# A gated cross-attention block with routed experts: the additions to the output wait for a product, and five steps stand later

## The chip, the cores and the metric

The kernel runs on one core of one Trainium2 chip. The metric is the device time of one execution in microseconds (us), as the median of several runs. The engines of the core work from queues of their own: TensorE (PE, whose weight loads are shown as PEld), VectorE (DVE), ScalarE (ACT), GpSimd (POOL) and SyncE (SP); they meet through semaphores. POOL and SP also issue the transfers (DMA).

## The reference, cut to what matters

32 batches of 112 rows of width 256 (3584 rows) go through two layers. In the first, each row looks at 375 context rows and at the normed rows themselves (8 heads of 64), and the result, times a gate, is added to x. In the second, each row is normed and sent to 2 of 8 experts, and the result, times a gate, is added too:

```python
x = x + jnp.tanh(g_xattn[0]) * xattn(ctx_1024, layernorm(x), mask, ...)
h = layernorm(x)
bids = sigmoid(h @ conf_w.T + conf_b) * wealth
top_bids, selected = jax.lax.top_k(bids, 2)            # 2 of E = 8 experts
weights = softmax(top_bids)
def ffn(gw, uw, dw):                                   # (1024,256), (1024,256), (256,1024)
    return (silu(h @ gw.T) * (h @ uw.T)) @ dw.T
x = x + jnp.tanh(g_ffn[0]) * sum(weights[e] * ffn_e(h) for the chosen e)
```

## The kernel before, in words

**Two stages.** The first 32 rounds (some 840 us) are the attention, one batch a round. The second stage is the experts' layer, which starts at about 855 us and is the one that the change touches. Its rows were scattered by expert into a buffer in HBM (`routed_rows`) and are taken up again in NT = 63 tiles of 128 rows. Each engine walks through the same loop `for t in range(1, NT + 1): step(t, ...)`, unrolled, each in its own written order; nothing but semaphores ties the engines together, and no planner moves anything.

**Precision by splitting.** A float32 matrix is held as two float16 halves (`hi` by ACT, `lo` by DVE), and `product` makes three matmuls for each block (hi·hi, hi·lo, lo·hi).

**One tile on PE** (`step`, L1792). `act_T(t-1, 1)` transposes the second half of the last tile's activations into `aP`; `tile_T(t+1)` transposes the next tile's rows into `xP`; `gate_up(t, q, 0)` makes the gate product and then the up product of the first 512 inner columns with the weights held in the array (48 matmuls of 128 columns, "weights held", tile names `gP<-xT,W` and `uP<-xT,W`); `gate_up(t, q, 1)` makes the other 512 inner columns with the rows held (12 matmuls of 512 columns, `gP<-W,xT` and `uP<-W,xT`, "the wide products"); `down(t-1)` makes the down product of the tile before (24 matmuls of 256 columns, `yP`). `gate_up(t, q, i)` adds one to `s_gu` at the end of its up product, so `s_gu` is 2t+1 after the products with weights held of tile t, and 2t+2 after the wide ones.

**Beside it.** In ACT's and DVE's step t stand, in this order: the hi and lo halves of the last tile's second activation half (`act_hi` L901, `act_lo` L1411, tile `aT<-aP`), of the next tile's rows (`tile_hi` L891, `tile_lo` L1396), then silu and the gated product of half 0 (`silu` L895, `gated` L1401), hi and lo of half 0 (`aT<-act_h`), silu and gated product of half 1. DVE then weighs the down product's rows (`weigh` L1417, tile `ysb`). POOL adds them to the output in HBM by an indirect, adding DMA (`add_tile` L637, DMA at L641). In POOL's step t the addition is that of tile t-1; `weigh(t-1)` comes after `down(t-1)` of PE's step t, so POOL's step t is worked through while PE is in its tile t+1. Before the addition POOL waits until the addition before it has landed (`s_add`, L668) and then issues the load of the rows of tile t+4 (`load_tile` L582, DMA at L587).

**The experts' weights.** They are loaded raw (float32, six pieces of 512 KB for an expert, `raw`), POOL issuing them in its steps after the addition: for experts 2 to 7 two pieces in each of three steps, those with t % 5 of 4, 0 and 1 (`FREE_AT`, `next_raw` L530). From the fifth expert on the split weights are also written to HBM (`put_pieces` L524). At the end of its steps ACT squares the pieces to find their size (`expert_squares` L845, tile `junk`): piece 0 in the step with t % 5 = 0, pieces 1 and 2 in the next, 3 to 5 in the one after. In the step with t % 5 = 3 PE sums the squares over the partitions (`expert_sums` L1651, `bP`), DVE makes a bound of them (`expert_bound` L1242), POOL takes the power -1/2 (`expert_pow` L518, `epow`), DVE makes the scale (`expert_scale` L1248), and ACT and DVE then split the pieces (`expert_hi` L856, `expert_lo` L1260, tile `W<-raw`).

**The start of the stage** (`tail`, L1694): PE works the first tile's products in between the last batch's output product, its norm's transposes (`norm2_T` L1626) and its routing confidences (`confidences` L1632). Tile 5 (the sixth; AHEAD = 5) is loaded only once the routing table is there, so its transposes stand later in step 4 than those of other tiles.

Matmuls are helper calls: line 1542 is `product`, 1773 `act_T`, 1737 `tile_T`, 1655 `expert_sums`.

Of the kernel before, what the change touches and what calls it, by code (L numbers as in the profile page):

```python
# [54 lines left out]
AHEAD = 5  # L55
# [35 lines left out]
def build(nc, x, ctxt, mask, scal, lnw, wqkv, wout, confw, confbw, wffn, out):  # L91
# [4 lines left out]
    with ctx:  # L96
# [220 lines left out]
        def holds(b, lo, hi):  # L317

            return lo <= b <= hi if isinstance(b, int) else True
# [121 lines left out]
        def _(pool):  # L441
# [76 lines left out]
            def expert_pow(p):  # L518

                pool.wait_ge(s_ech, p * ECHAIN + 2)  # L520
                apart(pool)
                nc.gpsimd.tensor_tensor(epow[:, :], ebound[:, :], minus_half[:, 0:3], ALU.pow).then_inc(s_epow, 1)
# [121 lines left out]
            def step(t, k):  # L644
# [30 lines left out]
                if p < E and t % SPAN == 3 and p > 1:  # L675
                    expert_pow(p)
                if holds(t, 1, NT):
                    add_tile(t - 1, (t - 1) % XT_BUFS)
# [21 lines left out]
        def _(act):  # L700
# [210 lines left out]
            def step(t, k):  # L911
# [17 lines left out]
                if t == AHEAD - 1:  # L929
                    tile_hi(t + 1, 1 - q)  # L930
                if t < NT:
                    if 0 not in TURNED:
                        act_hi(t, q, 0)
                    silu(t, 1, place)
                    if 0 in TURNED:
                        act_hi(t, q, 0)
# [30 lines left out]
        def _(dve):  # L967
# [455 lines left out]
            def step(t, k, place, last_place):  # L1423
# [13 lines left out]
                if t == AHEAD - 1:  # L1437
                    tile_lo(t + 1, 1 - q)
# [4 lines left out]
                if p < E and j == 3 and p > 1:  # L1443
                    expert_bound(p, bP)
                if t < NT:
                    gated(t, 1, place)
                    if 0 in TURNED:
                        act_lo(t, q, 0)
# [4 lines left out]
                if p < E and j == 3 and p > 1:  # L1453
                    expert_scale(p)
# [80 lines left out]
        def _(pe):  # L1535
# [158 lines left out]
            def tail():  # L1694
# [16 lines left out]
                gate_up(0, 0, 1, 0, (0,))  # L1711
                norm2_T(B - 1, (B - 1) % 4)
                gate_up(0, 0, 1, 0, (1,))
# [78 lines left out]
            def step(t, k, byte, last_byte):  # L1792
# [9 lines left out]
                if t == AHEAD - 1:  # L1802
                    tile_T(t + 1, (t + 1) % XT_BUFS)
                if SPAN < t and t // SPAN + 1 < E and t % SPAN == 3:
                    expert_sums(t // SPAN + 1, bP)
                if t == 1:
                    gate_up(t, q, 1, byte, (0,))
                    ranks(QUADS - 1, B * H, last_rank_P, last_tot_P)
                    gate_up(t, q, 1, byte, (1,))
                elif t < NT:  # L1810
                    gate_up(t, q, 1, byte)
                place = next_byte = None
# [60 lines left out]
```

## Time and profile before

| what | value |
| --- | --- |
| median of 3 runs | 1436.99 us (1432.22 to 1437.5) |
| the profiled execution | 1435.85 us, its span 1434.3 us |
| busy share of the span | PE 94%, PEld 68%, DVE 71%, ACT 65%, POOL 34% |
| mean granted TensorE clock | 0.989 of full speed |
| chain that ended last | PE 70%, DVE 10%, ACT 6%, issue 6%, DMA 5% |
| experts' stage, 960 to 1190 us | PE busy 226.17 of 230 us, DVE 138.54, ACT 135.04, POOL 87.76 |
| same, 1190 to 1250 us | PE busy 60.00 of 60 us |

The span is the stretch that the trace covers; the execution's own time is 1.55 us longer. In the rows, an x with a number gives how many instructions a row merges; what stands in brackets is the idle time of the engine before the row, and what ended it. "issue" is idle time for which the profile shows no releaser.

### The profile page before, as it was taken

The page shows a single profiled execution, that of the slowest core. Times are in us where ns is not written, and L with a number is a line of the kernel's source. Part 1 is how long each engine was busy: PE and PEld are TensorE (multiplying, and loading weights), DVE is VectorE, ACT ScalarE, POOL GpSimd, SP SyncE. Part 2 cuts the span into 40 slices and gives each one's busy share as a digit, 9 for nine tenths or more (in the row PEclk, how much of TensorE's full clock was granted, in tenths as well). Part 3 has the DMA queues.
Part 4 walks back from the last instruction along what each step waited for, and adds up shares of the span by engine and source line. Part 5 has one row for each costly group of instructions (what it writes and reads, how often), then busy time and mean ns, then how long its engine had stood idle before and what let it go on. Part 6 is the DMA issues. An engine that isn't in the chain of part 4 may idle for free.

```text
span 1434.3 us, 41525 instructions
## 1 busy us (share of the span) xinstructions
PE 1351.1 (94%) x13880; PEld 969.2 (68%) x13880; DVE 1023.5 (71%) x2528; ACT 934.8 (65%) x1932; POOL 488.2 (34%) x659
## 2 busy tenths in 40 slices
PE   2999999999999999999999979999999999999996
PEld 1466666666666666666665657688878778887784
DVE  4688888888888888888888776566556654444442
ACT  5687878787787878878787765566656663333331
POOL 4423322433433334334333143433344333222221
PEclk9999999999999999999999979999999999999998
DMA  4010101111111111111112146433376753112461
GB/s 119 27 42 26 42 23 29 52 40 49 34 53 30 41 46 39 49 33 53 31 33 96 41 129 196 107 98 93 98 211 178 228 152 94 31 31 35 120 203 16
DMA packets 56913, 109.26 MB, mean 76 GB/s; under 512 B 10832, under 2 KB 34768, under 8 KB 56720
## 3 DMA queue, kind: packets, MB, share of 16 engines
q0 software_dynamic: 23712, 55.71, 15.2%
q1 hardware_dynamic: 32160, 49.86, 11.2%
q8 instruction: 126, 2.06, 0.6%
q10 hardware_dynamic: 848, 1.07, 0.3%
q14 instruction: 67, 0.55, 0.1%
HBM read 69.16 MB, written 37.45 MB: 74 GB/s over the span
## 4 chain that ended last, share of the span: by engine, by line
PE 70%; DVE 10%; ACT 6%; issue 6%; DMA 5%; SPq 1%; POOL 1%; POOLq 0%; DVEq 0%; ACTq 0%
PE fP L1542 19%; PE yP L1542 10%; PE uP L1542 10%; PE gP L1542 10%; PE simP L1590 5%; PE ptP L1600 4%; PE tP L1542 3%; PE oP L1542 3%; DVE ms L1036 3%; DVE pT L1042 2%; DMA out<-ysb,xt 2%; PE aP L1773 2%; DVE ao L1054 1%; ACT z L732 1%; PE fP L1558 1%
## 5 line engine op out<-in xcount | busy, mean ns | idle before, releaser
L1542 PE MATMUL fP<-zTs,ws 128*128 128x112 f16 (+1 forms) x1536 | 220.3, 294 | 8.7 <-DVE zTs L1378 5.3
L1542 PE MATMUL fP<-ws,zTs 128*128 128x512 f16 x768 | 186.8, 379 | 0.5 <-DVE kT L1026 0.2
L1036 DVE CUSTOM_DVE_ANT_0 ms<-simP,madd,sim_undo 112x488 f32<-112x488 f32 x256 | 183.9, 720 | 3.3 <-PE simP L1590 1.3
L769 ACT ACTIVATE pr<-ms,nmax 112x488 f32<-112x488 f32 x256 | 179.0, 699 | 3.3 <-DVE nmax L1036 0.5
L1042 DVE SCALAR_TENSOR_TENSOR pT<-ptP,pT 122x448 f16<-122x448 f32 x256 | 157.8, 616 | 28.0 <-ACT pT L776 27.3
L1542 PEld LDWEIGHTS fP<-zTs,ws 128*128 128x128 f16 x1536 | 109.8, 99 | 99.7 <-issue 34.9
L1542 PE MATMUL yP<-W,aT 128*128 (+1 forms) x1512 | 175.4, 273 | 1.8 <-DVE aT L1414 1.8
L1542 PEld LDWEIGHTS yP<-W,aT 128*128 128x128 f16 x1512 | 147.6, 98 | 32.8 <-issue 2.5
L1408 DVE SCALAR_TENSOR_TENSOR act_h<-uP,consts,sg 128x512 f32<-128x512 f32 x126 | 94.5, 750 | 103.1 <-ACT sg L899 102.7
L776 ACT ACTIVATE pT<-ptP 122x448 f16<-122x448 f32 x256 | 137.8, 538 | 40.8 <-PE ptP L1600 39.7
L899 ACT ACTIVATE sg<-gP,consts 128x512 f32<-128x512 f32 x126 | 86.5, 686 | 114.6 <-PE uP L1542 114.4
L641 POOL DMA_INDIRECT out<-ysb,xt x63 | 105.2, 1670 | 157.4 <-DVE ysb L1421 143.8
L1542 PE MATMUL oP<-v,pT 122*128 122x64 f16 x3072 | 133.6, 194 | 14.0 <-DVE pT L1042 9.1
L1600 PE MATMUL ptP<-ident,pr 112*122 112x112 f32 x1024 | 142.0, 261 | 0.4 <-DVE filled L1148 0.4
L499 POOL TENSOR_TENSOR zTs<-zT,zTs 128x1200 f16<-128x1200 f32 x31 | 76.5, 2469 | 193.1 <-ACT zTs L750 193.1
L1542 PEld LDWEIGHTS oP<-v,pT 122*128 122x128 f16 x3072 | 121.0, 98 | 26.6 <-DVE pT L1042 26.5
L1600 PEld LDWEIGHTS ptP<-ident,pr 112*122 112x122 f32 x1024 | 114.2, 139 | 25.6 <-issue 0.8
L1542 PEld LDWEIGHTS fP<-ws,zTs 128*128 128x128 f16 x768 | 67.9, 98 | 82.1 <-issue 14.4
L1590 PE MATMUL simP<-kT,qT 64*128 64x488 f16 x768 | 102.7, 372 | 13.3 <-DVE nmax L1036 12.4
L1026 DVE SCALAR_TENSOR_TENSOR kT<-fP,kT 128x488 f16<-128x488 f32 x128 | 84.9, 664 | 37.2 <-ACT kT L762 37.2
L762 ACT ACTIVATE kT<-fP 128x488 f16<-128x488 f32 x128 | 73.8, 576 | 51.4 <-PE fP L1542 51.3
L1026 DVE SCALAR_TENSOR_TENSOR v<-fP,v 122x512 f16<-122x512 f32 x128 | 88.3, 690 | 26.5 <-ACT v L762 26.0
(233 smaller groups left out, 2496.2 us busy)
## 6 DMA issues: line engine op xcount, KB each, us to landing
raw<-wffn POOLq DMA_DIRECT2D x36, 512.0 KB, 6.9
split_experts<-W POOLq DMA_DIRECT2D x12, 1024.0 KB, 10.0
W<-split_experts SPq DMA_DIRECT2D x16, 768.0 KB, 7.9
xc<-ctxt SPq DMA_DIRECT2D x32, 375.0 KB
xt<-routed_rows POOLq DMA_DIRECT2D x63, 129.0 KB, 2.4
raw<-wffn SPq DMA_DIRECT2D x12, 512.0 KB, 9.5
routed_rows<-padrows SPq DMA_DIRECT2D x8, 645.0 KB, 7.9
xl<-x SPq DMA_DIRECT2D x32, 112.0 KB
```

Of the source, the lines that this page charges most:

```text
L499: nc.gpsimd.tensor_tensor(zTs[p][:, 1, :, :], zT[:, :, :], zTs[p][:, 0, :, :], ALU.subtract).then_inc(s_zsplit, 1)
L641: pool.indirect_dma_start(out[:, :], bass.IndirectOffsetOnAxis(ap=xt[k][:, D:D + 1].bitcast(I32), axis=0), ysb[t % 2][:, :], None, compute ...
L769: nc.scalar.activation(pr[h % 2][:, :], ms[h % 2][:, :], ACT.Exp, bias=nmax[p][:, h:h + 1], scale=-1.0, accum_out=rsum[p][:, h:h + 1]).the ...
L776: nc.scalar.activation(pT[h % 2][:, 0, :, 0:S], ptP[h % 2][0:KR, :, 0:S], ACT.Copy, scale=P_TOP).then_inc(s_pthi, 1)
L899: nc.scalar.activation(sg[i][:, :], gP[i][:, :], ACT.Silu, scale=constant(place, 0)).then_inc(s_silu, 1)
L1026: nc.vector.scalar_tensor_tensor(out=o, in0=i, scalar=1.0 / TOP, in1=hi, op0=ALU.mult, op1=ALU.subtract).then_inc(s_plo, 1)
L1036: nc.vector.tensor_tensor_reduce(out=ms[h % 2][:, :], in0=simP[h % 2][0:S, 0:NK], in1=madd[p][:, :], scale=sim_undo[0:S, 0:1], scalar=3.0e ...
L1042: nc.vector.scalar_tensor_tensor(out=pT[h % 2][:, 1, :, 0:S], in0=ptP[h % 2][0:KR, :, 0:S], scalar=P_TOP, in1=pT[h % 2][:, 0, :, 0:S], op0 ...
L1408: nc.vector.scalar_tensor_tensor(out=act_h[i][:, :], in0=uP[i][:, :], scalar=constant(place, 2), in1=sg[i][:, :], op0=ALU.mult, op1=ALU.mu ...
L1542: last = nc.tensor.matmul(o, lhs(k, a), rhs(k, c), start=n == 0, stop=n == len(todo) - 1)
L1590: last = nc.tensor.matmul(simP[i][:, 0:NK], qT[p][r, a, h // 2, :], kT[p][r, c, h // 2, :], start=t == 0, stop=t == len(PARTS) - 1)
L1600: last = nc.tensor.transpose(ptP[h % 2][0:KR, c, 0:S], pr[h % 2][:, c * KR:(c + 1) * KR], ident[0:S, 0:S])
```

## The change

- POOL, in its steps 6 to 61, waits before the addition of tile t-1 until `s_gu` is 2(t+1)+1, that is, until the up product with weights held of tile t+1 has ended.
- The sums of an expert's squares (`expert_sums`, experts 2 to 7) stand behind the wide products of PE's step instead of ahead of them; the bound (`expert_bound`) stands behind the second gated product of DVE's step, right ahead of the scale.
- In step 4 the transposes of tile 5, and their hi and lo halves on ACT and DVE, stand behind the wide products, the second silu and the second gated product.
- At the start of the stage the transposes of the last batch's norm stand behind all of `gate_up(0, 0, 1, 0)` instead of between its gate and its up product.

```diff
@@ POOL, step @@
                 if p < E and t % SPAN == 3 and p > 1:
                     expert_pow(p)
+                if AHEAD < t < NT - 1:
+                    pool.wait_ge(s_gu, (t + 1) * 2 + 1)
                 if holds(t, 1, NT):
                     add_tile(t - 1, (t - 1) % XT_BUFS)
@@ ACT, step @@
-                if t == AHEAD - 1:
-                    tile_hi(t + 1, 1 - q)
                 if t < NT:
                     if 0 not in TURNED:
                         act_hi(t, q, 0)
                     silu(t, 1, place)
+                    if t == AHEAD - 1:
+                        tile_hi(t + 1, 1 - q)
@@ DVE, step @@
-                if t == AHEAD - 1:
-                    tile_lo(t + 1, 1 - q)
                 if t < NT and 0 not in TURNED:
                     act_lo(t, q, 0)
                 if t == 2:
                     tile_places()
-                if p < E and j == 3 and p > 1:
-                    expert_bound(p, bP)
                 if t < NT:
                     gated(t, 1, place)
+                    if t == AHEAD - 1:
+                        tile_lo(t + 1, 1 - q)
...
                 if p < E and j == 3 and p > 1:
+                    expert_bound(p, bP)
                     expert_scale(p)
@@ PE, tail @@
                 gate_up(0, 0, 0, 0, (1,))
-                gate_up(0, 0, 1, 0, (0,))
+                gate_up(0, 0, 1, 0)
                 norm2_T(B - 1, (B - 1) % 4)
-                gate_up(0, 0, 1, 0, (1,))
                 confidences(B - 1)
@@ PE, step @@
                 if 1 < t < NT:
                     gate_up(t, q, 0, byte)
-                if t == AHEAD - 1:
-                    tile_T(t + 1, (t + 1) % XT_BUFS)
-                if SPAN < t and t // SPAN + 1 < E and t % SPAN == 3:
-                    expert_sums(t // SPAN + 1, bP)
...
                 elif t < NT:
                     gate_up(t, q, 1, byte)
+                if t == AHEAD - 1:
+                    tile_T(t + 1, (t + 1) % XT_BUFS)
+                if SPAN < t and t // SPAN + 1 < E and t % SPAN == 3:
+                    expert_sums(t // SPAN + 1, bP)
```

## Rows read from the trace of the kernel before

**Rows 1.** The table of waits, 900 to 1430 us: total us, times, longest.

```profile
ACT junk L854 <- DMA raw<-wffn: 31.2, 19, 4.7
PE bP L1655 <- ACT junk L854: 3.2, 3, 1.4
```

**Rows 2.** The timeline of tiles 22 and 23: start us, length us, engine, line, what.

```profile
1056.73 0.60 PE L1773 MATMUL aP<-ident,act_h 128*128 128x128 f32 x4
1057.39 1.50 PE L1542 MATMUL gP<-xT,W 128*128 128x128 f16 x24
1058.46 1.66 POOL L641 DMA_INDIRECT out<-ysb,xt  x1 [0.95 <-DVE ysb L1421]
1058.73 1.50 PE L1542 MATMUL uP<-xT,W 128*128 128x128 f16 x24
1059.23 1.06 ACT L854 ACTIVATE junk<-raw 128x1024 bf16<-128x1024 f32 x1 [3.20 <-DMA raw<-wffn]
1059.51 1.74 POOL L534 DMA_DIRECT2D raw<-wffn  x2
1060.07 1.46 PE L1542 MATMUL gP<-W,xT 128*128 x6
1060.29 0.58 ACT L909 ACTIVATE aT<-aP 128x512 f16<-128x512 f32 x1
...
1065.28 0.60 PE L1773 MATMUL aP<-ident,act_h 128*128 128x128 f32 x4
1065.54 0.56 POOL L587 DMA_DIRECT2D xt<-routed_rows  x1 [3.58 <-issue]
...
1067.69 1.06 ACT L854 ACTIVATE junk<-raw 128x1024 bf16<-128x1024 f32 x1 [2.79 <-DMA raw<-wffn]
```

**Rows 3.** The timeline of tile 31 and the start of tile 32.

```profile
1137.66 0.60 PE L1773 MATMUL aP<-ident,act_h 128*128 128x128 f32 x4
...
1142.68 0.58 ACT L909 ACTIVATE aT<-aP 128x512 f16<-128x512 f32 x1
...
1147.17 0.63 PE L1773 MATMUL aP<-ident,act_h 128*128 128x128 f32 x4 [0.28 <-issue]
```

**Rows 4.** The timeline of tile 8 (starts at 934.33) and tile 9: the power and the scale.

```profile
936.06 1.65 POOL L641 DMA_INDIRECT out<-ysb,xt  x1 [2.94 <-DVE ysb L1421]
...
941.18 0.57 POOL L587 DMA_DIRECT2D xt<-routed_rows  x1 [3.47 <-issue]
...
942.71 0.17 DVE L1251 TENSOR_SCALAR ebits<-epow 128x3 int32<-128x3 int32 x1 [0.36 <-POOL epow L522]
...
943.24 0.60 PE L1773 MATMUL aP<-ident,act_h 128*128 128x128 f32 x4
...
946.26 0.57 ACT L909 ACTIVATE aT<-aP 128x512 f16<-128x512 f32 x1
```

**Rows 5.** A window: us, busy PE, PEld, DVE, ACT, POOL, granted clock, DMA, GB/s.

```profile
901.50:904.50 3.00, 3.00 (x8) 1.06 (x7) 0.91 (x2) 0.27 (x1) 2.24 (x2) 0.50 0.54 92
```

**Rows 6.** The timeline of steps 4 and 5, around the sixth tile.

```profile
900.40 0.44 PE L1737 MATMUL xP<-ident,xt 128*128 128x128 f32 x2 [2.85 <-DMA xt<-routed_rows]
...
902.26 1.48 POOL L522 TENSOR_TENSOR epow<-ebound,minus_half 128x3 f32<-128x3 f32 x1
...
906.54 0.16 DVE L1251 TENSOR_SCALAR ebits<-epow 128x3 int32<-128x3 int32 x1
...
912.23 0.69 DVE L1414 TENSOR_TENSOR aT<-aP,aT 128x512 f16<-128x512 f32 x1
```

**Rows 7.** The groups by line, 840 to 1434 us: busy us, mean ns, idle before.

```profile
L1542 PE MATMUL uP<-xT,W 128*128 128x128 f16 x1512 | 99.1, 219 | 0.0
L1542 PE MATMUL gP<-xT,W 128*128 128x128 f16 x1512 | 96.7, 221 | 0.0
```

**Rows 8.** The timeline of POOL and PE in tile 30.

```profile
1132.46 1.46 PE L1542 MATMUL gP<-W,xT 128*128 x6
...
1132.84 1.60 POOL L641 DMA_INDIRECT out<-ysb,xt  x1 [0.30 <-issue]
```

## The prediction, made before the changed kernel was run

> **What bounds the kernel now.** I read the busy shares first, then the windows of the experts' stage: there PE has work nearly all the time (the table above: 226 of 230 us, then 60 of 60). So in this stage the time is PE's work plus what little PE waits, and a step is worth only what it takes from or adds to that. Then the timeline of one tile after another. An ordinary tile on PE is 8.55 to 8.7 us: from the transposes of `aP` to the products with weights held 0.66, gate 1.34 (1057.39 to 1058.73), up 1.34 (in other tiles to 1.5), the two wide products 2.59 and down 2.62 (together 1060.07 to 1065.28) [rows 2]. The table of waits has hardly a PE row: 3.2 us behind ACT's squares, three times [rows 1]. But ACT waits 31.2 us, 19 times, for the raw weights [rows 1]. That is the wait to watch, since ACT's squares stand ahead of the halves that PE's next down product needs.
>
> How late may ACT be? Tile 31 shows it: `aT<-aP` starts 5.02 us after the tile's start on PE, the tile lasts 9.51 instead of 8.57, and the next `aP` starts 4.49 after ACT's row [rows 3]. In between lie, one behind the other, ACT's halves and silu, DVE's gated product, the halves of half 0 and the second gated product; so PE stands still from a lateness of 8.57 - 4.49 = 4.1 us on, and each us above costs a us. In tile 22 the lateness is 3.56 [rows 2] and nothing stalls. I call this number the lateness of a tile.
>
> **Part 1, the wait ahead of the addition.** Before, the addition starts 1.73 us into the tile (1058.46) [rows 2], within the up product with weights held. Now it waits for that product's end, 3.34 into the tile. The start behind a semaphore took 0.8 us here when DVE's `ysb` was what it waited for, and PE's end is seen 0.15 us later; so 4.3 us, 2.6 later than now. POOL's queue behind it is: the raw pieces, the write of split weights, the wait for the landing, the load of rows for tile t+4, the power. The load of rows has three tiles to spare and costs nothing. POOL's own round fits: addition to load is 7.1 us in the fullest tiles (1058.46 to the load at 1065.54, [rows 2]), in a tile of 8.6.
>
> What it can gain: the addition's 1.65 us lie on the up product now. Counted by groups, up with weights held is busy 99.1 us and gate 96.7 [rows 7], 2.4 apart; by the distances of starts the 51 undisturbed up products of tiles 7 to 61 take 1.34 to 1.62 against 1.34, 4.3 us in sum, some of it with a full overlap at 1.34. In the wide products an addition costs nothing, by the one tile where it fell there: 1.46 as always [rows 8]. Gain between 0 and 4.3, taken as 3. The Trainium skill, "SBUF — State Buffer", section "SBUF: two separate sides", says that engine ports and DMA ports are disjoint, so that neither slows the other; by it this gain would be 0 and the sum 3 us higher. The trace leaves it open: up takes 1.34 in tile 22 under a whole addition [rows 2], and up to 1.5 in other tiles.
>
> What it costs, first: raw pieces. They start 1.05 us behind the addition (1059.51), so 5.4 into the tile instead of 3.0 or 2.8 (3.5 to 4.8 in four tiles where they are late today). The piece that is waited for lands 5.4 to 8.2 us after its issue (1059.51 to 1067.69, [rows 2]; 5.4 to 6 where no split weights are written), and ACT squares it as soon as it is there: in tile 22 it waited 3.20 for it and began `aT<-aP` 1.06 later [rows 2]. Every such lateness grows by 2.0 to 2.6 us. The pattern stands 18 times (six experts, three tiles each); lateness before and shift, with the stall of the tile ahead taken off where it lets the piece come earlier in the tile:
> - tile 8: 2.7 + 2.6 = 5.3, stall 1.2; tile 13: 1.8 + 2.6, 0.3; tile 18: 2.5 + 2.6, 1.0;
> - tile 21: 3.0 + 2.0, 0.9; tile 22: 3.56 + 2.5 - 0.9, 1.1; tile 23: 4.7 + 2.6 - 1.1 = 6.2, 2.1, of which 1.5 are there now;
> - tile 26: 3.0 + 2.4, 1.3; tile 28: 4.8 + 2.5, 3.2, of which 1.6 now;
> - tile 31: 5.0 + 1.1, 2.0, of which 0.95 now; tile 33: 4.1 + 1.8, 1.8, of which 0.9 now; the other eight nothing.
> Sum 1.2 + 0.3 + 1.0 + 0.9 + 1.1 + 0.6 + 1.3 + 1.6 + 1.05 + 0.9 = 10 us.
>
> Second: the power waits on POOL for the landing of the addition in the same tile. Now 936.06 to the load at 941.18 is 5.1, to DVE's `ebits` 942.71 another 1.5 [rows 4]. From 4.3 this gives 10.9 into the tile instead of 8.4. The scale, ACT's three splits and DVE's two follow, and lateness of tile 9 is 946.26 - 943.24 = 3.02 [rows 4]. Less the length that the tile ahead has gained, it grows by 1.0 to 2.4 in the six tiles behind a scale: stalls of 0.75 (tile 9), 1.3, 0.9, 1.1, 0.95, 0.9, together 5.9 us.
>
> **Part 2, sums and bound later.** The sums go from ahead of the wide products to behind them; the 0.2 us of their two matmuls stay. PE's three waits of 1.1, 1.4 and 0.7 us there [rows 1] go, but the same late ACT holds the down product after them, so they are in the "now" of tiles 23, 28 and 33 above and not taken twice. The bound comes after the second gated product, 8.1 into the tile (0.35 long), and is there before POOL is free at 10.0; only in stalled tiles does it decide, which is in the 5.9. Cover gone: DVE no longer has 0.75 us of gated product beside the power, and waits; what is behind it is `weigh` (needed by the next down product, 3 us of air). In itself 0; if POOL were free it would cost 0.75 x 6 = 4.5 at most, and at best the sums give back their 3.2.
>
> **Part 3, the sixth tile.** PE waits 2.85 us for the rows of tile 5, [rows 6], and after that the granted clock is 0.50 [rows 5], so that the wide products take 2.2 and 2.1 instead of 1.3 each (six matmuls in 1.3 in tile 22, [rows 2]). Moved, the wide products run in the wait, and the transposes start at 900.40 as the load lands, whatever PE did before. Step 5 would begin at 900.40 + 0.27 + 2.62 = 903.3 instead of 907.57. What is late next is the power at 902.26 to 903.74 [rows 6], bound to POOL: `ebits` comes at 903.8 instead of 906.54, 2.8 earlier, and DVE's `aT<-aP` of 912.23 comes at 909.5, 6.2 into step 5. It stalled nothing at 4.7, so PE gives back 1.4. Gain 2.8; at least 1.5 if PE's shorter wait halves the clock once more, at most 4.3.
>
> **Part 4, the last norm later.** PE idled before these transposes and now works the up product in that time, about 1.5 us. But all PE steps up to 900.40 end in the wait for the sixth tile's load, and that hangs on SP's and POOL's transfers, not on PE. So 0; were that cover gone, 1.5 gained.
>
> **The last tiles.** POOL's steps 62 and 63 don't wait; the addition before them lands 1 us ahead of its need. 0.
>
> **Sum.** 1435.85 + 10 + 5.9 - 3 - 2.8 = 1446. The profiled execution lies 1.1 us below the median of the three runs, so the median may be 1446 to 1447; I say 1446.
>
> **Rivals.**
> - *The raw weights come in time* (faster). If landing is set by the transfers and not by the issue, later pieces meet emptier queues and land when they did; the power too has room. Then only the gains stay: 1435.85 - 3 - 2.8 = 1430. For it: pieces beside a write of split weights took 8.2 us, others 5.4 to 6, so traffic matters. Against it: the addition's neighbours shift with it, so the crowd shifts too, and in experts 2 to 4 there is no crowd. It decides from where landing takes 2.5 us less than now. The Trainium skill, "DMA: Bandwidth & Descriptors", section "Anatomy of one DMA — SWDGE (gpsimd) path", gives 2.0 us plus bytes / 436e3; for 512 KB that is an estimate of 3.2 us, with which no piece would be late and this rival would hold. The trace speaks against it: 8.2 us [rows 2].
> - *Half of it*: the limit of 4.1 is taken from one tile; if 0.5 more is in it, the 16 stalls lose 8 us: 1438.
> - *Nothing moves*: the wait is mostly met, additions start as before; 1436 - 2.8 = 1433. Against it: 1.73 is 1.6 ahead of the product's end [rows 2].
> - *The clock falls in the new stalls*: PE stands 1.3 to 1.4 us twice in tile 28. Waits of 1.1 and 1.4 [rows 1] were followed by wide products of 1.3, that of 2.85 by the clock of 0.50 [rows 5, 6]. If three stalls do, at 1.7 each as in step 4: 1451.
>
> **Chances.** Stalls as worked out, with or without the clock: 0.60 (of it 0.08 with). Half: 0.15. In time: 0.15. Nothing moves: 0.10. About 0.5%, 7.2 us, is what can be told from no change. Slower by more: most of the first case, 0.53; within: half and nothing, and the ends of both others, 0.33; faster: 0.14. Range 1431 to 1452; that of the likeliest alone 1442 to 1452.
>
> **What would show it.** Additions at 4.3 us into tiles 7 to 62; raw pieces at 5.4; ACT's waits for raw grown from 31 to some 60 us; tiles 8, 18, 21, 22, 26, 28 longer by 1 us and more, the tiles behind a scale by 0.8 to 1.3; up with weights held at 1.34 throughout; tile 40 and later shorter by 0.1 each; step 5 at 903.3. It is wrong if ACT's wait for raw does not grow, or the late tiles keep 8.6 us.

## The result, and the profile after

| | before | changed kernel |
| --- | --- | --- |
| median | 1435.69 us (1432.22 to 1437.5, 5 runs) | 1456.66 us (1455.9 to 1457.71, 5 runs) |
| ratio | | 1.0143 [1.0129, 1.0157] |
| profiled execution | 1435.85 us, span 1434.3 | 1455.9 us, span 1454.0 |
| PE busy, 960 to 1190 us | 226.17 of 230 | 222.31 of 230 |
| granted clock over the span | 0.989 | 0.992 |

The change is slower by 21 us; I had forecast 10, with a range up to 1452. In kernel.py the lines behind L676 carry numbers up to two higher than before. The table of waits of the changed kernel, 900 to 1450 us (total us, times, longest), answers [rows 1]:

```profile
POOL out L641 <- PE uP L1543: 145.3, 47, 7.0
...
ACT junk L856 <- DMA raw<-wffn: 55.3, 20, 5.1
...
PE yP L1543 <- DVE aT L1416: 7.0, 8, 1.5
...
PE aP L1773 <- DMA W<-split_experts: 1.9, 1, 1.9
PEld bP L1656 <- ACT junk L856: 0.9, 3, 0.4
```

The wait is real (47 additions now wait for `uP`), ACT's wait for raw weights grew from 31.2 to 55.3 us, and PE's waits for the squares are gone. But PE's own waits sum to about 12 us, those it had before included, and the span grew by 20. The timeline of tile 22 (starts at 1065.19), which answers [rows 2] and [rows 3], shows the rest:

```profile
1065.19 0.63 PE L1773 MATMUL aP<-ident,act_h 128*128 128x128 f32 x4 [0.28 <-issue]
...
1065.87 1.74 PE L1543 MATMUL gP<-xT,W 128*128 128x128 f16 x24
...
1067.50 1.97 PE L1543 MATMUL uP<-xT,W 128*128 128x128 f16 x24
1068.88 1.06 ACT L856 ACTIVATE junk<-raw 128x1024 bf16<-128x1024 f32 x1 [3.56 <-DMA raw<-wffn]
1069.37 1.46 PE L1543 MATMUL gP<-W,xT 128*128 x6
...
1070.37 1.66 POOL L641 DMA_INDIRECT out<-ysb,xt  x1 [3.19 <-PE uP L1543]
...
1071.42 1.74 POOL L534 DMA_DIRECT2D raw<-wffn  x2
...
1074.58 0.60 PE L1773 MATMUL aP<-ident,act_h 128*128 128x128 f32 x4
```

From gate to up is 1.63 us and from up to the wide gate product 1.87, where tile 22 of before had 1.34 and 1.34, and PE is busy all the while: the tile is 0.84 longer without a stall. The same in tile 10, behind the first late scale (`ebits` 2.1 us into tile 9 instead of 8.4 into tile 8; this answers [rows 4]):

```profile
942.14 0.57 POOL L587 DMA_DIRECT2D xt<-routed_rows  x1 [3.47 <-issue]
...
943.74 0.17 DVE L1253 TENSOR_SCALAR ebits<-epow 128x3 int32<-128x3 int32 x1 [1.93 <-POOL epow L522]
...
947.29 0.57 ACT L911 ACTIVATE aT<-aP 128x512 f16<-128x512 f32 x1
...
950.93 0.74 DVE L1410 SCALAR_TENSOR_TENSOR act_h<-uP,consts,sg 128x512 f32<-128x512 f32 x1
...
951.77 0.63 PE L1773 MATMUL aP<-ident,act_h 128*128 128x128 f32 x4 [0.23 <-issue]
...
952.46 1.80 PE L1543 MATMUL gP<-xT,W 128*128 128x128 f16 x24
...
954.15 2.03 PE L1543 MATMUL uP<-xT,W 128*128 128x128 f16 x24
...
956.07 1.46 PE L1543 MATMUL gP<-W,xT 128*128 x6
```

Tile 9 keeps my rule (lateness 947.29 - 941.63 = 5.66, length 10.14 = 5.66 + 4.48). Tile 10 has no late row at all and is 9.51 long instead of 8.66. What is different is where DVE's second gated product ends: 951.67, 0.10 us before PE's `aP`; in an undisturbed tile it is 0.94 to 0.95 before. I call that distance the lead. The groups by line, 840 to 1454 us, answer [rows 7]: up with weights held grew by 7.7 us, gate by 3.6.

```profile
L1543 PE MATMUL uP<-xT,W 128*128 128x128 f16 x1512 | 106.8, 218 | 0.9 <-issue 0.7
...
L1543 PE MATMUL gP<-xT,W 128*128 128x128 f16 x1512 | 100.3, 220 | 0.1
```

The sixth tile, against [rows 5] and [rows 6]: the window's granted clock is 1.00 now, the transposes start at 901.27, and step 5 at 904.86 instead of 907.57.

```profile
900.00:904.50 4.50, 3.97 (x29) 2.66 (x28) 1.98 (x4) 1.59 (x3) 3.46 (x4) 1.00 0.41 95
```

```profile
901.27 0.44 PE L1737 MATMUL xP<-ident,xt 128*128 128x128 f32 x2
...
903.23 1.48 POOL L522 TENSOR_TENSOR epow<-ebound,minus_half 128x3 f32<-128x3 f32 x1
...
904.74 0.17 DVE L1253 TENSOR_SCALAR ebits<-epow 128x3 int32<-128x3 int32 x1 [1.61 <-POOL epow L522]
904.86 0.60 PE L1773 MATMUL aP<-ident,act_h 128*128 128x128 f32 x4
```

### The profile page after: what moved, and what is told of

Its sections match the earlier page's. It is cut to its first block and busy times, and to the rows that moved or that the text cites. A ratio compares the mean times of both kernels' runs of the same rounds, so it can differ in the third digit from the quotient of the medians.

```text
span 1454.0 us, 41531 instructions
## 1 busy us (share of the span) xinstructions
PE 1365.2 (94%) x13880; PEld 975.1 (67%) x13880; DVE 1021.5 (70%) x2528; ACT 931.5 (64%) x1932; POOL 486.8 (33%) x659
## 5 line engine op out<-in xcount | busy, mean ns | idle before, releaser
L1543 PEld LDWEIGHTS yP<-W,aT 128*128 128x128 f16 x1512 | 147.0, 98 | 39.0 <-issue 10.3
L1591 PE MATMUL simP<-kT,qT 64*128 64x488 f16 x768 | 101.9, 369 | 13.4 <-DVE nmax L1038 10.6
L1543 PE MATMUL uP<-xT,W 128*128 128x128 f16 x1512 | 106.8, 218 | 0.9 <-issue 0.7
L1028 DVE SCALAR_TENSOR_TENSOR v<-fP,v 122x512 f16<-122x512 f32 x128 | 88.2, 689 | 26.5 <-ACT v L764 26.4
```

Of the source, the lines that this page charges most:

```text
L1028: nc.vector.scalar_tensor_tensor(out=o, in0=i, scalar=1.0 / TOP, in1=hi, op0=ALU.mult, op1=ALU.subtract).then_inc(s_plo, 1)
L1543: last = nc.tensor.matmul(o, lhs(k, a), rhs(k, c), start=n == 0, stop=n == len(todo) - 1)
L1591: last = nc.tensor.matmul(simP[i][:, 0:NK], qT[p][r, a, h // 2, :], kT[p][r, c, h // 2, :], start=t == 0, stop=t == len(PARTS) - 1)
```

## The experiments

Times stand beside those of before on the same chip. "Excess" is the length of tiles 7 to 35 above 8.55 us each, from distances of starts on PE in the profiled execution: 10.3 before, 29.3 after.

### Which part of the change costs: the wait

**e1**: before with the wait alone.

```
                 if p < E and t % SPAN == 3 and p > 1:
                     expert_pow(p)
+                if AHEAD < t < NT - 1:
+                    pool.wait_ge(s_gu, (t + 1) * 2 + 1)
```

> The kernel before with the new wait alone (POOL's steps 6 to 61 wait for the next tile's up product with weights held before the addition); nothing is moved. Theory (A): the wait alone makes raw pieces and power late, and a late ACT costs twice: the tile lasts lateness + 4.49 us, and where the second gated product is ready less than 0.3 us before PE takes it up, the next tile's products with weights held take some 0.85 us more. Then this run carries the whole loss of the change and lacks the 2.7 us that its step 4 gains: 1456 to 1460 us, some 19 tiles with weights-held products of 3.4 us and more instead of 2.7 to 2.8. Rival (B): the later sums and bound are what costs: 1446 or less, as forecast for the wait's own part.

Measured 1464.02 us against 1436.6, ratio 1.0196 [1.0168, 1.0225], excess 32.9; that is above the 1456 to 1460 that I expected, and made up otherwise: besides the tiles in which PE waits for squares, 7 of tiles 7 to 35 have held products above 3.3 us, not the 19 expected. ("Held products" are the gate and up products with weights held, both together.) The sums ahead of the wide products turn late squares into PE waits (13.1 us in the table of waits, 3.2 before), and in tiles 23, 28 and 33 the clock falls behind them. In tile 23 PE waits from 1079.8 to 1082.4, and the wide products take 2.48 and 1.79 us instead of 1.29 each. The window behind the wait has a granted clock of 0.62 (columns as in [rows 5]):

```profile
1077.94 1.89 PE L1544 MATMUL uP<-xT,W 128*128 128x128 f16 x24
1082.42 0.39 PE L1657 MATMUL bP<-esq,ones 128*128 128x6 f32 x2 [2.59 <-ACT junk L856]
1082.67 2.69 PE L1544 MATMUL gP<-W,xT 128*128 x6
1085.15 1.95 PE L1544 MATMUL uP<-W,xT 128*128 x6
```

```profile
1082.50:1087.00 4.50, 4.50 (x15) 1.79 (x16) 2.66 (x6) 1.83 (x4) 0.96 (x2) 0.62 0.34 62
```

So beside the wait the other parts together save about 7 us.

**e2**: the changed kernel without the wait (the two added lines of e1 taken out).

> The changed kernel without the new wait; sums, bound, sixth tile and last norm stand later. (A): step 4 gives 2.7 us; raw pieces start at 1.7 + 1.1 into the tile again. The bound now ends 8.5 us into the tile, so the scale comes about 1 us later than before in six tiles, lateness 3.0 grows to 4.0 to 4.4 there: stalls of 0 to 0.3 and a slow next tile each, 3 to 6 us in all. 1434 to 1440. (B): 1446 or more.

Measured 1438.17 against 1436.6, ratio 1.0012 [0.9999, 1.0026], excess 11.2. So nearly all of the 21 us are the wait's: 18.5 by the medians, 18.8 by the ratios.

**e9** and **e11**, and further down **e13** and **e14**: the changed kernel with fewer waits, by the condition on the wait:

```
e9:  if AHEAD < t < NT - 1 and (t % SPAN == 3 or t > 35):
e11: if 35 < t < 52:
e13: if AHEAD < t < 36 and t % SPAN == 2:
e14: if AHEAD < t < 36 and t % SPAN in (4, 0, 1):
```

> After, with the wait kept only in the 33 steps where neither a raw piece of weights nor the power of a scale is queued behind the addition or behind its landing: steps 8, 13, 18, 23, 28, 33 (tiles 9, 14, ... 34) and steps 36 to 61. Theory A (the wait costs only by what is queued behind it): as the kernel without the wait, 1438.2, plus up to 0.5 us per expert for raw pieces that come 0.4 us later and up to 2 us at tiles 60-61, where the reload of the last expert's place meets it: 1438 to 1442. Rival W (the wait costs by itself, or the late landing does through the tile's rows): the 18.5 us of 56 waits shared out evenly are 0.33 us for each, 33 of them 11 us: 1447 to 1450.

> After, with the wait only in steps 36 to 51 (tiles 37 to 52). In after and in the kernel with 33 waits tile 60 is 10.7 and 10.1 us long, with PE waiting 1.4-2.0 us for the reload of the eighth expert's place. Theory T (late additions in the last tiles beside the reload slow it): with no waits from step 52 on, tile 60 is back at 8.7 and the kernel stands at 1438 as without any wait, so 16 waits cost nothing. Rival (what makes the reload late lies further ahead): tile 60 stays over 10 us and the time is 1440.

e9: 1437.7 against 1436.29, ratio 1.001 [0.9996, 1.0025]; e11: 1437.41 beside 1438.02 (one run). A late addition costs nothing where nothing is queued behind it, and gains nothing either: tiles 36 to 59 together are 1.6 us above 8.55 each in before and 1.9 in the changed kernel. That the last tiles suffer from it did hold for e11 (tile 60 at 8.67), but e12 and e13 below have no wait there and tile 60 at 9.88 and 9.82, e16 10.69. Whether the reload of the eighth expert's place comes in time varies without the wait; the +2.2 us of that kind in the changed kernel's profile are not shown to be its doing.

**e13** and **e14**: the wait only in the six steps ahead of a scale, and in the 18 with raw pieces.

> After, with the wait only in steps 7, 12, 17, 22, 27, 32 (tiles 8, 13, 18, 23, 28, 33), where the power of the scale is taken behind this addition's landing and no raw piece is behind it. Theory A (the late landing makes the scale late): ebits 1.3-3 us into tiles 9, 14, 19, 24, 29, 34 instead of 0.4-1.0, those tiles 0.5 to 2 us longer than without the wait, 6 to 8 us in all, 1444 to 1446.5. Rival (the scale is late by the raw pieces' lateness, so this wait alone does little): 1438 to 1441.

> After, with the wait only in the 18 steps up to 35 whose raw pieces of weights are issued behind the addition (t mod 5 = 4, 0, 1; tiles 10-12, 15-17, ... 35). Theory A (the costs of the wait are two separate ones, and add up: 18.5 in all, 10.8 in the steps ahead of a scale, 0 in the quiet tiles): 1443 to 1448, raw pieces at 5.4 us, the squares late in tiles 11-13, 16-18, 21-23, 26-28, 33 as in after, ebits in tiles 9, 14 back at 0.4 us. Rival (they are one: the raw pieces' lateness costs only where the scale is late as well): 1438 to 1441.

e13: 1450.27 against 1438.02, ratio 1.0087 [1.0063, 1.0111], excess 22.5; e14: 1453.17 against 1435.81, ratio 1.0115 [1.0093, 1.0136], excess 26.4. Both cost more alone than I expected, and both rivals fall; but their excess is 11.3 and 15.2 us above that of e2, and that of the changed kernel, which has both, only 18.1. In e13, tile 24, where the squares are in time, the power follows the landing and the load, and PE stands 1.73 us:

```profile
1083.08 0.57 POOL L587 DMA_DIRECT2D xt<-routed_rows  x1 [4.11 <-issue]
...
1083.68 0.91 POOL L522 TENSOR_TENSOR epow<-ebound,minus_half 128x3 f32<-128x3 f32 x1
1084.69 0.17 DVE L1253 TENSOR_SCALAR ebits<-epow 128x3 int32<-128x3 int32 x1 [3.53 <-POOL epow L522]
...
1089.71 2.78 PE L1543 MATMUL yP<-W,aT 128*128 x24 [1.73 <-DVE aT L1416]
```

In e14, where the landing is in time, `ebits` still comes 1.35 us into tiles 9, 14, 19, 24, 29 and 34, not 0.4: the late squares hold the second gated product of the tile ahead, and the bound stands behind it. The scale is late by either way, so the two costs overlap.

### Can the queue behind the wait be repaired

**e15**: the changed kernel with the power taken ahead of the landing. **e3**: raw pieces and writes of split weights issued ahead of the wait. **e4**: both.

```
+                if p < E and t % SPAN == 3 and p > 1:      # e15, e4
+                    expert_pow(p)
                 if holds(t, 2, NT):
                     pool.wait_ge(s_add, t * 16 - 16)
...
+                if t > AHEAD:                               # e3, e4
+                    pieces()      # next_raw(...), put_pieces(...) of this step
                 if AHEAD < t < NT - 1:
                     pool.wait_ge(s_gu, (t + 1) * 2 + 1)
```

> After, with the power of a scale taken on GpSimd ahead of the wait for the addition's landing; all waits and raw pieces as in after. Theory A (the scale is late by the landing alone): ebits in tiles 9, 14, 19 at 0.4 us instead of 2.1-3.2, hi at about 3.9 instead of 5.7-6.7; tiles 9, 14 and 19 at 8.6 instead of 10.1-11.2, tiles 24, 29 and 34 shorter by 0.5 to 1; the tiles behind keep their slow products with weights held: 1456.7 less 6 to 11, 1446 to 1451. Rival (in tiles 23, 28 and 33 GpSimd now waits for a late bound, and its next load and addition get later): 1452 to 1458.

> The changed kernel, with the raw pieces and the writes of split weights issued ahead of the new wait (POOL's steps from 6), the addition where the change puts it. (A): the pieces start about 1.5 us into the tile instead of 5.4, ACT's waits for raw fall from 55 us to under 31, and the stalls of the tiles with t % 5 of 1, 2, 3 go, those of the kernel before as well; the power still waits for the landing, so tiles 9, 14, 19, 24, 29, 34 still last 9.4 to 11 us and the ones behind them are slow: 1440 to 1446. Rival (C), the later additions themselves hold PE up by their traffic or by the time they take: 1454 or more, slow weights-held products as before this edit.

> As the run with the raw pieces first, and POOL takes the power before it waits for the landing of the last addition and loads rows. (A): the scale is then bound by the later bound alone, 9.5 us into the tile instead of 11; the six tiles behind it lose 0 to 1.2 us each with what follows: 1432 to 1439, near the kernel before although every addition is still 2.6 us late. (C): 1450 or more.

e15: 1451.88 against 1435.81, ratio 1.0107 [1.0085, 1.0129]; 5 us less than the changed kernel, just above the 1446 to 1451 that I expected. `ebits` falls from 2.1, 2.5 and 3.2 to 1.3, 0.7 and 1.3 us and does not reach 0.4, for the reason of e14. e3: 1477.02 against 1436.6, ratio 1.0281 [1.0255, 1.0308]. ACT's wait for raw weights fell to 16.4 us, as meant, but in the experts whose split weights are written back, the pieces and the write now stand ahead of the addition; from such an addition to the load behind its landing it is 6.4 to 10.1 us instead of 4.8 to 6.9 in the same steps of the changed kernel, additions come up to 12.6 us apart, and the power waits for all of it: tiles 24, 29 and 34 take 17.6, 17.6 and 16.7 us. Its waits:

```profile
ACT W L873 <- DVE escale L1261: 46.0, 7, 10.5
...
PE yP L1550 <- DVE aT L1423: 27.4, 11, 7.2
```

e4: 1462.68 against 1436.6, ratio 1.019 [1.0162, 1.0218]. Tiles 9, 14 and 19 are back at 8.54 to 8.57 (`aT<-aP` at 3.91), and the tiles behind them still 9.25 to 9.37; tiles 23, 28 and 33 take 14.5, 15.1 and 16.8. GpSimd's round of addition, landing and load is longer than a tile there, which I take for the cause; no run tries it alone. All three forecasts of a repaired kernel missed: in each of the three orders tried the late addition holds something up.

### The slow products without a stall

In e2 tiles 10 and 15 were 9.35 and 9.31 us long behind tiles of 8.57 and 8.55 with `aT<-aP` at 3.9, that is below my limit of 4.1. So I tested the lead by itself.

**e5**: before, and VectorE wastes time ahead of the second gated product in tiles 38 to 52.

```
+                    if t in LATER:    # 352, 512, 640, 768, 896 columns, three tiles each
+                        n = LATER[t]
+                        nc.vector.tensor_tensor(spent[:, 0:n], raw[:, 0:n], raw[:, n:2 * n], ALU.add)
                     gated(t, 1, place)
```

> Before, with one waste addition on VectorE (352, 512, 640, 768, 896 columns in tiles 38-40, 41-43, 44-46, 47-49, 50-52) ahead of the second gated product; it moves no data by DMA and touches nothing that PE reads. The second gated product there ends 0.94 us before PE starts the transposes of the next tile's step, after an idle time of VectorE of 0.23 us. Theory L (a tile is slow when that lead is under about 0.3 us): tiles 39 to about 47 stay at gP 1.34 and uP 1.34-1.5; once the lead falls under about 0.3 us, with 768 or 896 columns (tiles 48-53), gP held takes 1.5-1.8 and uP held 1.86-2.05, so 0.75-0.95 us more per tile, with a granted clock of 1.00 and with no wait of PE for the gated product. Rival D (the held products were slow because of the DMA traffic or the clock of the busy stretch): all of tiles 39-53 stay at 2.7-2.9 us for both held products as long as PE does not wait, and the time is that of before within 1 us. By L it is 3 to 6 us longer, 1440 to 1443.

The run took 1436.79 us beside 1436.29 (one run; its tile 38 began 4.4 us sooner than in before, and tiles 39 to 53 gave back 5.1). The lead does it, with no transfer and no stall, but not as I put it: there is no edge at 0.3, the products lengthen with each step. Tile 53, lead 0.32:

```profile
1328.07 1.08 DVE L1450 TENSOR_TENSOR spent<-raw 128x896 f32<-128x896 f32 x1
...
1329.08 0.74 DVE L1410 SCALAR_TENSOR_TENSOR act_h<-uP,consts,sg 128x512 f32<-128x512 f32 x1
1330.14 0.60 PE L1778 MATMUL aP<-ident,act_h 128*128 128x128 f32 x4
...
1330.80 1.60 PE L1547 MATMUL gP<-xT,W 128*128 128x128 f16 x24
...
1332.29 1.97 PE L1547 MATMUL uP<-xT,W 128*128 128x128 f16 x24
1334.16 0.81 PE L1547 MATMUL gP<-W,xT 128*128 x3
```

From the gated product's end, 1329.82, to the end of the held products, 1334.16, is 4.34 us. That distance is the same everywhere:

| lead, us | tiles | held products, us | gated product's end to their end, us |
| --- | --- | --- | --- |
| 0.09 to 0.30 | 19 of the changed kernel | 3.55 | 4.36 |
| 0.32 to 0.48 | 6 of e5 | 3.27 | 4.32 |
| 0.59 to 0.60 | 3 of e5 | 3.05 | 4.30 |
| 0.94 to 0.95 | 35 of the changed kernel | 2.77 | 4.37 |

So the held products end no sooner than 4.36 us after PE's wait for the gated product is met. In between PE has 54 matmuls (4 and 2 transposes, 48 products), each with its load of weights: 4.36 / 54 = 81 ns for a pair, where products that have been queued up run at 1.34 / 24 = 56 ns. In single tiles the distance is 4.2 to 4.5 us. A stream of instructions that can't pass a wait would do this, and it would be counted by the instruction:

**e10**: before, with 4, 8, 16 and 24 waits that are long met, behind the transposes of tiles 38 to 41, 42 to 45, 46 to 49 and 50 to 53.

```
+                for _ in range(MET.get(t, 0)):
+                    pe.wait_ge(s_const, 1)
                 if 1 < t < NT:
                     gate_up(t, q, 0, byte)
```

> Before, with 4, 8, 16 and 24 waits for a semaphore that was met long ago, on PE between the tile's transposes and its products with weights held, in tiles 38-41, 42-45, 46-49 and 50-53. They compute nothing, and VectorE and ScalarE are as in before (lead 0.94 us). In all traces so far the products with weights held end 4.36 us (4.28 to 4.5) after the second gated product, whatever the lead between 0.1 and 0.95 us. Theory Q (PE's sequencer takes 54 matmuls and their weight loads in those 4.36 us, 81 ns for each pair, some 40 ns for an instruction, and the gated product's end is where it starts): each added instruction moves the end by about as much; at 40 ns the two held products go from 2.8 to about 2.95, 3.1, 3.4 and 3.75 us though nothing is late, the distance from the gated product grows to 4.5, 4.7, 5.0 and 5.3 us, and the run is 5 to 8 us longer. Rival E (the floor is not in the instructions' number; it is the gated product, or what DVE writes then, that disturbs the engine): held products stay at 2.7-2.9 us and the time that of before within 1 us.

Measured 1450.83 beside 1438.02 (one run). VectorE's lead stays at 0.95, and the distance grows from 4.3 to 4.4 in these tiles of before to 4.6, 4.8 to 4.9, 5.2 to 5.3 and 5.6 to 5.7: 50 to 65 ns for each wait, more than the 40 that I took. (The excess of tiles 36 to 59 grew by 11.4 us for 208 waits, 55 ns each.) Rival E, by which nothing would lengthen, falls. Tile 47:

```profile
1283.34 0.75 DVE L1409 SCALAR_TENSOR_TENSOR act_h<-uP,consts,sg 128x512 f32<-128x512 f32 x1 [0.29 <-ACT sg L900]
1285.03 0.60 PE L1774 MATMUL aP<-ident,act_h 128*128 128x128 f32 x4
...
1285.69 1.74 PE L1543 MATMUL gP<-xT,W 128*128 128x128 f16 x24
...
1287.33 2.10 PE L1543 MATMUL uP<-xT,W 128*128 128x128 f16 x24
1289.33 1.02 PE L1543 MATMUL gP<-W,xT 128*128 x4
```

**e16** and **e17**: the wait and its transposes between the two held products, in before with the sixth tile and the last norm moved (e16) and in the changed kernel (e17).

```
-                act_T(t - 1, 1)
+                if not 1 < t < NT:
+                    act_T(t - 1, 1)
                 if t < NT - 1 and t != AHEAD - 1:
                     tile_T(t + 1, (t + 1) % XT_BUFS)
                 if 1 < t < NT:
-                    gate_up(t, q, 0, byte)
+                    gate_up(t, q, 0, byte, (0,))
+                    act_T(t - 1, 1)
+                    gate_up(t, q, 0, byte, (1,))
```

> Before, with the sixth tile and the last norm moved (1434.4 alone), and on PE the transposes of the second gated product, with the wait for it, between the gate and the up product with weights held instead of ahead of both. Theory Q (held products end 4.36 us after the gated product because PE's instructions behind that wait can't be issued sooner; now 24 of the 48 are issued ahead of it): gP held and uP held 1.34 each in nearly all tiles, quiet tiles 8.54 instead of 8.55-8.7, no tile behind a late one slow; in before the two held products took 8 us (tiles 7-35) and 1.8 (36-59) more than 2.68 each: 1425 to 1430. Rival (ScalarE and VectorE get the transposed product 1.6 us later, their chain of copies becomes what PE waits for): 1434 to 1445.

> The changed kernel with the same reordering of PE as in the run before this one; the addition and all that waits behind it stay late. Theory Q: of its +21 us against before, the products with weights held (16.6 us above 1.34 each in tiles 7-35, 2.1 in 36-59, 0.9 in 61) go, the stalls by late squares and scales stay: 1436 to 1442. Rival E (the slow held products come from late work on ScalarE and VectorE and not from the order on PE): 1452 to 1458.

e16: 1429.09 against 1435.81, ratio 0.9949 [0.9932, 0.9965], by its median the fastest kernel of the case (e18 and e19 below can't be told from it by their ratios). Of that 0.51%, e8 below, which has the two moved parts without the reordering, has 0.17. Tiles 36 to 59 are 8.55 or 8.56 each, without exception; before they were 8.54 to 8.74. Tile 41:

```profile
1221.45 0.38 PE L1736 MATMUL xP<-ident,xt 128*128 128x128 f32 x2
1221.67 1.50 PE L1542 MATMUL gP<-xT,W 128*128 128x128 f16 x24
...
1223.01 0.60 PE L1772 MATMUL aP<-ident,act_h 128*128 128x128 f32 x4
...
1223.45 1.50 PE L1542 MATMUL uP<-xT,W 128*128 128x128 f16 x24
...
1224.79 1.46 PE L1542 MATMUL gP<-W,xT 128*128 x6
```

The rival's cost, ScalarE's copy at 2.2 instead of 0.64 us into the tile, appears and holds nothing up. e17: 1446.85 against 1435.81, ratio 1.0069 [1.0044, 1.0094]: of 1.43% the reordering takes 0.74%, some 10.6 us. That is less than the 15 to 20 of the theory, since where PE stalls anyway the slow products had been hidden in the stall: PE's wait for `aT` at the down product, 7.0 us in the changed kernel, is 11.7 here, and the late tiles stay long (tile 19: 10.91, tile 28: 12.44). Both rivals fall.

### The other parts, and the best of them

**e7**: before with only the sums of squares behind the wide products. **e8**: before with only the sixth tile and the last norm moved. **e12**: e8 with the power ahead of the landing.

> Before, with only the sums of squares moved on PE from ahead of the wide products to behind them (bound and power stand where they were in before). Theory A (the sums' waits for late squares are the 4.5 us that the change took away, and the bound ahead of the gated product costs nothing since the sums are done at 6.2 us and the gated product starts at about 6.9): tiles 23, 28 and 33 fall from 10.3, 10.4 and 9.7 to 8.7-8.9, the scales come as in before (tiles 9, 14 at 8.7, 24, 29, 34 under 8.8), total 1430.5 to 1434. Rival B (the later bound pushes the gated product of tiles 8, 13, 18, 23, 28, 33 back, the lead falls under 0.3 us and the tiles behind pay 0.8 each): 1436 to 1439.

> Before, with only the sixth tile's transposes and splits later in step 4 and the last norm's piece later (no wait, sums and bound as in before). In the profiled runs steps 3 and 4 together took 22.05 us before, 20.28 after and 22.16 in the kernel without the wait, which has the same step 4 as after. Theory A (the gain of 1.9 us in the changed kernel's profile was chance, what ends step 4 is the table that the whole chip of work waits for): 1435.5 to 1438 where before has 1436.6, same within 0.1%. Rival B (the move gains what I forecast, 2 to 2.8 us): 1433.5 to 1435.

> Before, with the sixth tile and the last norm moved as in the faster kernel (1434.4), and the power of a scale taken on GpSimd ahead of the wait for the addition's landing instead of behind it and a tile's load. Theory A (tile 19's scale comes late only because its power waits for the landing of the addition behind two writes of split weights): ebits of the scale in tile 18 instead of 0.46 us into tile 19, tile 20's held products at 2.8 instead of 3.5; 0.7 us less than the kernel with the sixth tile alone, 1433.0 to 1435.0. Rival B (GpSimd waits there for the bound, the load and the addition come later, and the raw pieces with them): 1435 to 1438.

e7: 1435.67 against 1436.29, ratio 0.9992 [0.9979, 1.0006], where I had expected 4 us less: PE's wait for late squares goes, but `aT<-aP` is as late as it was (4.96 us in tile 23), and DVE's bound, which still stands ahead of the second gated product and takes 0.4 us, now falls into the lead: it is 0.10 in tiles 24, 29 and 35 and 0.62 in tile 34, and these take 9.2 to 9.5. e8: 1434.38, ratio 0.9983 [0.997, 0.9996]: 2.4 us less, and between 0.6 and 4.3, so rival B fits, and the gain that I forecast for the sixth tile (2.8) is within it, the last norm's share included. e12: 1435.58 against 1438.02, ratio 0.9983 [0.9972, 0.9993]: tile 20 is at 8.55 as expected, and the whole no faster than e8.

**e18**: e2 with the split of e16; **e19**: that with the power first.

> The changed kernel without its wait (1438.2 against 1436.6 for before) and with the transposes of the second gated product between the two held products. It differs from the kernel at 1429.1 only in the sums of squares behind the wide products and the bound behind the second gated product. Theory Q: tiles 23, 28 and 33, which took 10.43, 10.40 and 10.03 us there, fall to about 8.7; tiles 19, 24, 29 and 34 gain 0.1 to 0.5 each by their later scales, but the tiles behind them stay at 8.55: 3 to 5 us less than 1429.1, 1424 to 1426.5. Rival (the late scale costs as much with the split as without it): 1428.5 to 1431.

> As the run before this one, with the power of a scale taken on GpSimd ahead of the wait for the addition's landing. Theory A: the scales of tiles 19, 24, 29 and 34 come 0.3 to 0.6 us earlier, which is worth 0.5 to 1.5 us: 1423 to 1426. Rival (GpSimd waits for the late bound of tiles 23, 28 and 33 and its loads and raw pieces come later): up to 2 us longer than the run before this one.

e18: 1432.18 against 1438.27, ratio 0.9955 [0.994, 0.9971]; e19: 1430.96, 0.9953 [0.9937, 0.9969]; e16 had 0.9949. Tiles 23, 28 and 33 are 4.7 us shorter than in e16, as expected, but tiles 24, 25, 29, 30, 31 and 35 are 4.2 longer: the later scale holds the addition, and the raw pieces behind it come late (tile 31: 10.54). My theory that the split would keep the gain of the later sums was wrong: the sums' gain is given back through GpSimd's queue, and not only through the slow products.

## Why the prediction was wrong

By tiles, changed kernel less before, in the profiled executions (spans 1454.0 and 1434.3):

| term | forecast, us | measured, us |
| --- | --- | --- |
| raw pieces: tiles 8, 13, 18, 21, 22, 23, 26, 28, 31, 33 | +10 | +4.3 |
| power and scale: tiles 9, 14, 19, 24, 29, 34 | +5.9 | +8.5 |
| the tiles behind late ones: 10, 15, 17, 20, 25, 27, 30, 35 | 0 | +5.8 |
| the rest of tiles 7 to 35 | 0 | +0.4 |
| additions off the up product | -3 | +0.3 (tiles 36 to 59) |
| sixth tile, up to the start of tile 7 | -2.8 | -1.8 |
| the last tiles | 0 | +2.2 |
| sum | +10.1 | +19.7 |

**The step that failed** is "PE stands still from a lateness of 4.1 us on", used as if lateness had no other price, with "the other eight nothing" and nothing for the tiles behind late ones, which took 5.8 us. As a rule for the late tile it held (tile 19: 6.72 + 4.49 = 11.21, measured 11.21). But from a lateness of about 3.3 in a tile of 8.55 the second gated product comes closer than 0.94 us to PE's `aP`, and the held products of the next tile lengthen by as much, up to 0.85 us. Such pairs were in the trace of before: tile 19 has `aT<-aP` at 4.07 and length 8.68, tile 20 nothing late and 9.37. The tile behind tile 31, from which I took the 4.1, is another: it takes 9.52, with a lead of 0.11 and gate and up at 1.72 and 1.91.

```profile
1146.32 0.74 DVE L1408 SCALAR_TENSOR_TENSOR act_h<-uP,consts,sg 128x512 f32<-128x512 f32 x1
1147.17 0.63 PE L1773 MATMUL aP<-ident,act_h 128*128 128x128 f32 x4 [0.28 <-issue]
...
1147.85 1.82 PE L1542 MATMUL gP<-xT,W 128*128 128x128 f16 x24
...
1149.57 2.01 PE L1542 MATMUL uP<-xT,W 128*128 128x128 f16 x24
...
1151.48 1.45 PE L1542 MATMUL gP<-W,xT 128*128 x6
```

I had looked at stalls only, and a slow product is no idle time. Thirteen tiles of the changed kernel (10, 13, 15, 17, 20, 22, 24, 25, 27, 30, 32, 34, 35) have hardly any excess but this; the table books some of them under the raw pieces and the scale. Counted by kind instead of by tile, about 11 of the 19.0 us of tiles 7 to 35 are the held products (7.7 and 3.6, the groups by line), and by this estimate about 8 are left for stalls, where I had forecast 15.9. e5, e10, e16 and e17 show the mechanism.

**Raw pieces.** The mechanism was right (pieces at 5.4 us and later, ACT's wait 55 us against the 60 forecast), and the size was too large: tiles 8, 18, 28 and 31 were forecast 4.9 us longer together and came out 0.9 shorter. In tile 31 the lateness even fell from 5.02 to 4.04 though the piece was issued 1.5 us later in tile 30: tile 30 itself was 0.9 longer, and ACT began on the piece 6.0 us after its issue instead of 7.7. What shortened the landing was not tried.

**Power and scale.** 8.5 against 5.9; here the late squares delay the scale as well (e14), which I had left out.

**Additions off the up product.** The gain of 3 does not exist. Up with weights held kept its 1.34 to 1.54 us in quiet tiles with the addition behind it, in most of them to 0.05 us the same tile by tile (tile 39 takes 8.63 in both kernels, tile 56 8.74), and falls to 1.34 in all of them when part of the products stands ahead of the wait (e16). The 4.3 us that I had read as the addition's weight on the product are the same floor: with a lead of 0.95, products at 1.34 each end 4.29 us after the gated product, and the floor in these tiles is 4.28 to 4.48. Why it differs from tile to tile is open. By the Trainium skill, "SBUF — State Buffer", section "SBUF: two separate sides", this gain was to be 0, and the measurement agrees; I had it beside the sum and let the rows' other reading stand.

**Sums and bound**: taken at 0 in itself, which e2 and e7 bear out; e1 shows what I did not say: without the moved parts the wait costs about 7 us more, of which e8 gives some 2.4 to the sixth tile and the last norm, so that the rest, 4 to 5, falls to this part. **Sixth tile**: -1.8 in the profile and -2.4 by e8, forecast -2.8. The transposes came at 901.27, not 900.40, as the load was later. **Last norm**: not tried alone. **Last tiles**: +2.2 from the reload, which varies by itself.

**The rivals.** "The raw weights come in time" fell with ACT's wait of 55 us. "Half of it" had 8 us for the stalls, which is near what they came to, but not for its reason: the limit of 4.1 held. "Nothing moves" fell with the additions at 4.4; the granted clock did not fall in the stalls of the changed kernel (1.00 in the windows around tiles 19, 23, 26, 28 and 33), but did in e1, behind PE waits of 2.6 to 3.7 us. None of them had the mechanism that decided.

## What to carry to other kernels

A semaphore wait in the stream of PE acted here as a point that its instructions can't pass. Where many short matmuls follow it, the time from the wait's release to their end has a floor of its own, and it costs before anything stalls; look for groups whose duration varies between tiles although their engine is never idle, and put short matmuls that don't need what the wait is for ahead of it, as e16 does. Before delaying an issue on a queue, list what stands behind it and behind its landing: here a wait that costs nothing where the queue is empty cost about 11 us of excess in six steps ahead of a power and 15 in eighteen ahead of raw pieces.

## What the runs showed of the hardware

- The floor (changed kernel, e5): 54 pairs of weight load and matmul of 128 columns end 4.36 us (4.2 to 4.5) after the wait ahead of them is met, 81 ns for a pair; queued pairs run at 56 ns. The Trainium skill, "TensorE: Matmul & The Clock Gate", section "Back-to-back issue gap", gives about 81 ns for a matmul of 128 columns in a stream of loads and matmuls. The trace agrees with that behind a late wait, and shows less where the instructions could be queued ahead.
- A wait on PE that is met already took 50 to 65 ns of the stream (e10). What within PE sets the 81 ns for a pair was not separated; e10 shows that instructions without a load or a matmul lengthen the stream too.
- An indirect addition of 128 rows beside the held products costs them nothing that these runs can show (e9, e11: 32 and 16 of them moved, same time).
- An addition to the output behind the raw pieces and a write of split weights on the same queue took 6.4 to 10.1 us to the load that waits for its landing, 4.8 to 6.9 in the same steps with them behind it (e3, changed kernel).
